# Final norm of a graph layer and expert feed-forward kernel: statistics of the last tile to ScalarE, scaling of tiles four and five to ScalarE and GpSimd's transfers

## What is computed

```python
edge_index = jnp.stack([src, dst])
x = x + _L0_gnn_ref(_layernorm(x, axis=-1), edge_index, W, b)
x = x + _L0_ffn_ref(_layernorm(x, axis=-1)[None], router_w, router_b, w1, b1, w2, b2, ln_w, ln_b)[0]

# the end of _L0_ffn_ref: out is the weighted sum of the experts
out = out.reshape(b, s, h) + hidden_states
return _layernorm(out, ln_w, ln_b)      # eps 1e-12, mean and variance over the 1024 columns
```

## Time and profile before

| what | value |
|---|---|
| median of 3 runs | 615.42 us (614.85 to 615.75) |
| the profiled execution, its own time | 617.8 us |
| its span, first to last instruction | 615.7 us |
| PE, DVE, ACT, POOL busy share of the span | 87%, 75%, 39%, 32% |
| DMA, mean rate over the span | 182 GB/s |
| mean granted TensorE clock | 0.954 of full |
| last expert add issued by GpSimd | 574.61 us |
| last matmul issued | 572.20 us |

### The profile page before, as it was taken

One profiled execution on the slowest core, in us unless ns is written; L12 is line 12 of the kernel. 1 busy time (PEld: TensorE's weight loads), 2 busy tenths in 40 slices (PEclk: granted clock), 3 DMA queues, 4 the chain that ended last, 5 costly groups with the idle time before them and its releaser, 6 DMA issues.

```text
span 615.7 us, 12330 instructions
## 1 busy us (share of the span) xinstructions
PE 533.8 (87%) x3660; PEld 298.8 (49%) x3661; DVE 464.7 (75%) x1295; ACT 243.0 (39%) x358; POOL 194.4 (32%) x199
## 2 busy tenths in 40 slices
PE   1799999899999999995879999999999999999100
PEld 1344554445544555553764655556565656564000
DVE  8889869996185888888748678695868685755397
ACT  5334444323271434342634343444443444401480
POOL 3023000000001375746434535343453444151240
PEclk9999999999999999997789999999999999999755
DMA  6873531243237334346367959698888889273878
GB/s 237 322 289 100 155 89 25 56 78 65 50 140 271 137 139 172 138 171 204 90 262 203 296 164 256 217 238 274 208 251 207 258 230 281 29 168 77 264 209 278
DMA packets 59581, 112.34 MB, mean 182 GB/s; under 512 B 33506, under 2 KB 33919, under 8 KB 59520
## 3 DMA queue, kind: packets, MB, share of 16 engines
q1 hardware_dynamic: 49440, 80.02, 37.4%
q0 software_dynamic: 8896, 27.38, 21.3%
q10 hardware_dynamic: 1184, 4.20, 1.9%
HBM read 71.75 MB, written 33.67 MB: 171 GB/s over the span
## 4 chain that ended last, share of the span: by engine, by line
PE 77%; DVE 14%; issue 4%; DMA 3%; ACT 1%; DVEq 0%; ACTq 0%; SPq 0%; POOLq 0%
PE ps L1818 7%; PE ps L1819 7%; PE ps L1943 7%; PE ps L1944 6%; PE ps L1945 6%; PE ps L1922 6%; PE ps L1923 5%; PE ps L1924 5%; PE ps L1728 5%; PE ps L1729 4%; PE ps L1730 4%; PE ps L1655 4%; PE ps L1904 4%; DMA acc_rows<-work,ids_out 1%; DVE wbufs L1574 1%
## 5 line engine op out<-in xcount | busy, mean ns | idle before, releaser
L615 POOL DMA_INDIRECT acc_rows<-work,ids_out x24 | 53.0, 2206 | 107.6 <-DVE work L1510 107.6
L1922 PE MATMUL ps<-rows_and_counts,wbufs 128*128 128x336 f16 (+2 forms) x256 | 76.1, 301 | 3.0 <-issue 2.2
L1924 PE MATMUL ps<-rows_and_counts,wbufs 128*128 128x336 f16 (+2 forms) x256 | 76.1, 301 | 0.0
L1923 PE MATMUL ps<-rows_and_counts,wbufs 128*128 128x336 f16 (+2 forms) x256 | 76.1, 301 | 0.0
L1819 PE MATMUL ps<-wbufs,rows_and_counts 128*128 128x512 f16 x200 | 75.8, 379 | 0.0
L1818 PE MATMUL ps<-wbufs,rows_and_counts 128*128 128x512 f16 x200 | 75.8, 379 | 0.0
L1943 PE MATMUL ps<-wbufs,rows_and_counts 128*128 (+1 forms) x192 | 72.9, 380 | 1.8 <-issue 1.3
L1465 DVE SCALAR_TENSOR_TENSOR wbufs<-stage,wbufs 128x1024 f16<-128x1024 f32 x56 | 67.1, 1218 | 8.1 <-ACT wbufs L933 7.6
L1944 PE MATMUL ps<-wbufs,rows_and_counts 128*128 (+1 forms) x192 | 72.8, 379 | 0.0
L1945 PE MATMUL ps<-wbufs,rows_and_counts 128*128 (+1 forms) x192 | 72.8, 379 | 0.0
L528 POOL TENSOR_TENSOR work<-work 128x1024 f16<-128x1024 f32 x9 | 19.2, 2132 | 164.3 <-ACT work L906 164.3
(11 more groups left out here) (310 smaller groups left out, 1050.5 us busy)
## 6 DMA issues: line engine op xcount, KB each, us to landing
stage<-wst_in SPq DMA_DIRECT2D x72, 512.0 KB
acc_rows<-work SPq DMA_DIRECT2D x10, 512.0 KB
x_rows<-work SPq DMA_DIRECT2D x10, 512.0 KB
wbufs<-b_in ACTq DMA_DIRECT2D x8, 512.0 KB
wbufs<-acc_rows SPq DMA_DIRECT2D x8, 512.0 KB, 5.9
t<-x_in SPq DMA_DIRECT2D x1, 3584.0 KB, 13.2
t<-x_in SPq DMA_DIRECT2D x1, 3072.0 KB, 11.3
t<-x_in SPq DMA_DIRECT2D x1, 2048.0 KB, 7.8
```

The costliest lines, as they stand in the source:

```text
L1922: mm(o, wbufs[:, ds(w + ws, P)], x_hi, start=(j == 0), stop=False)
L1923: mm(o, wbufs[:, ds(w + ws, P)], x_lo, start=False, stop=False)
L1924: ins = mm(o, wbufs[:, ds(w + (LO + ws), P)], x_hi, start=False, stop=(j == DK - 1))
```

## The change

ScalarE takes the statistics of tile 9 too, so VectorE has no statistics of its own in the third group. `ADDED` grows from tiles 0 to 3 to tiles 0 to 5 and `WHOLE` shrinks to tiles 6 to 9: tiles 4 and 5 are stored as `t` early, scaled by ScalarE at line 1027 and added onto `out` by GpSimd's line 647, and are neither passed over by VectorE's line 1612 nor stored by SyncE's line 745. GpSimd waits for six landed stores of `t` in place of four. Neither the groups nor the order of the waits on the other lines changes.

```diff
-ACT_TILES = (0, 1), (4, 5), (8,)
-ADDED = LAST_GROUPS[0]
-WHOLE = LAST_GROUPS[1] + LAST_GROUPS[2]
+ACT_TILES = (0, 1), (4, 5), (8, 9)
+ADDED = LAST_GROUPS[0] + LAST_GROUPS[1][:2]
+WHOLE = LAST_GROUPS[1][2:] + LAST_GROUPS[2]
...
                 act.wait_ge(rstd5_done, n + 1)
-                for r in tiles:
+                for r in [r for r in tiles if r in ADDED]:
                     act.wait_ge(weighed, r + 1)
                     a.activation(fin[r], fin[r], ACT.Copy, scale=rstd5[:, r:r + 1]).then_inc(scaled, 1)
...
-                own = tiles
-                if n < len(ACT_TILES):
-                    own = tiles[len(ACT_TILES[n]):]
-                cs = slice(own[0], own[-1] + 1)
+                own = tiles[len(ACT_TILES[n]):]
                 for r in own:
                     dve.wait_ge(fin_in[r], 16)
                     st5.did(v.bn_stats(stats5[:, r, 0:6], fin[r][:, 0:HALF]))
                     st5.did(v.bn_stats(stats5[:, r, 6:12], fin[r][:, HALF:D]))
+                if own:
+                    cs = slice(own[0], own[-1] + 1)
+                    st5.wait()
+                    for r in own:
+                        st5.did(v.bn_aggr(mv5[:, r, :], stats5[:, r, :]))
+                    st5.wait()
+                    st5.did(v.tensor_scalar(var5[:, cs], mv5[:, cs, 1], EPS2, None, ALU.add))
+                cs = slice(tiles[0], ACT_TILES[n][-1] + 1)
+                dve.wait_ge(square5_done, n + 1)
+                ins = v.tensor_scalar(var5[:, cs], square5[:, cs], EPS2, None, ALU.add)
                 st5.wait()
...
-                if tiles[0] in WHOLE:
+                if tiles[-1] in WHOLE:
                     dve.wait_ge(x1b_done, NT)
                     dve.wait_ge(rstd5_done, n + 1)
-                    for r in tiles:
+                    for r in [r for r in tiles if r in WHOLE]:
                         dve.wait_ge(weighed, r + 1)
                         v.scalar_tensor_tensor(fin[r], fin[r], rstd5[:, r:r + 1], t[:, r * D:(r + 1) * D],
                                                ALU.mult, ALU.add).then_inc(finished, 1)
```

More of the change, by code:

```diff
@@ L1585, in _ @@
                     st5.did(v.bn_stats(stats5[:, r, 6:12], fin[r][:, HALF:D]))
-                st5.wait()
[L1587 to L1596, removed]
+                if own:
[8 more added lines that the diff above has]
+                ins = v.tensor_scalar(var5[:, cs], square5[:, cs], EPS2, None, ALU.add)
+                st5.wait()
                 ins.then_inc(var5_done, 1)
```

## The result

Six runs of the changed kernel gave a median of 623.70 us (622.57 to 625.25), six of the kernel before 615.59 us (613.46 to 618.07). The ratio is 1.0138 with a 95% interval of 1.0113 to 1.0163: 8.5 us slower, where I had forecast 1.7.

The account below looks back on a forecast made before the run. The DMA engines were to become the bound: two adds cost 5.2 us, two stores fewer give 2.5, and VectorE's 4 us only fill a gap. That made 1.7 us more, 617.1 us, range 615.3 to 618.5.

Parts of the forecast that it names:

- 4.0 us forecast: VectorE in the tail: two final passes fewer give 2.39 us, tile 9's statistics and the first small addition 1.63.
- both covers: ScalarE's slack before VectorE needs its results: 1.8 us for tile 9's sums, 0.9 us for the third group's root.
- the early part: Two more early stores of `t` on SyncE: forecast to cost nothing, at most 1 us by delaying GpSimd's expert-weight gathers.
- the fourth rival: Early stores push the gathers past VectorE's read, last expert's results up to 1 us late: 618.1 us, chance 0.07.
- the queue never runs dry: GpSimd's queue: tile 4's add is queued by 604.7, while the fourth add runs until 607.1; issue time costs nothing.
- 23.2 us to the last byte: DMA engines: data end at 616.25, counted from the first add's issue at 593.07.
- the price of an add: DMA engines: an accumulating tile takes 2.6 us at 0.20 MB/us, a plain store 1.25 us.
- the filled gap: The DMA engines' wait for VectorE between 611.1 and 612, under one us, was to be filled with work.
- The 1.2 us: Stretch from the last data at 614.54 to the span's end at 615.7, carried over unchanged to the changed kernel.
- my own sum: DMA work after 603.4: 1.58 MB of adds (7.8 us) plus 2.10 MB of stores (5.05 us), 12.85 us.
- the reading from which I began: Two resources nearly level in the tail, VectorE and the DMA engines; the change relieves the first and loads the second.
- The faster rival: Adds hold the DMA engines no longer than plain stores, VectorE's 4.0 us come off in full: 611.4 us, chance 0.08.

## Why the prediction was right in its direction and wrong in its size

VectorE: right. 4.0 us forecast and 4.02 found.

ScalarE: right. Its statistics, scalings and root came, set against the first add's issue, within 0.1 us of the forecast, and both covers held.

SyncE and the early part: the two early stores were put at nothing, with up to 1 us as the other end, and cost 0.6 us ahead of the tail. The path wasn't the one forecast: VectorE's read of the expert weights isn't late, TensorE's matmul of line 1943 is. Of the fourth rival the effect came true, the last expert's results late, and not its cause.

GpSimd's issues: the two new ones began 8.8 and 11.2 us after the first, forecast 9.6 and 11.9. I had given them a start-up of 1.1 us that only the first has. But "the queue never runs dry" was wrong, as the fifth add's data didn't move until 605.7.

The DMA engines: the size was right, 23.2 us to the last byte forecast and 23.4 found; so were the price of an add (2.6 us of engine time, with 0.42 MB/us for the plain transfers as the contrast) and the filled gap. That the total came out within 0.2 us is in part luck, as the order was another: tiles 8 and 9 weren't stored beside the adds from 604.16 on, but 4.7 us later.

The step that failed is the one behind it: "Now they end at 614.54 and the span at 615.7, 1.2 us later. So the span becomes 616.25 + 1.2." I took SyncE's last store for the only end, because the chain of waits closed on VectorE's last pass, whose result that store carries, and SyncE's last long wait was for that store. The 1.2 us held GpSimd's drain, which ended 0.4 us after SyncE's stream by coincidence, having begun at 608.2. That drain follows the last add, not the last byte. Put into my own sum it gives the result: the adds' data would end at about 603.4 + 1.58/0.143 = 614.5 (0.143 MB/us being the adds' share of both queues, 0.53 MB in 3.7 us), they land 0.9 us later as before (607.1 to 608.0), and 7.7 us on the span ends at 623.1, 7.4 over before against 8.1 found. Of the 0.7 left, 0.5 is a later landing and 0.2 a longer way from landing to end (7.9 us in place of 7.7); whether the pause is behind the 0.5 isn't shown. So of a loss of 8.1 us in the tail, my mechanism, the engines' work, carries 2.0 (the last byte), and the drain that had been hidden behind VectorE and the stores carries 6.1.

The same row overturns the reading from which I began. It was not VectorE and the DMA engines that were level in the tail of the kernel before, but SyncE's end, which both of these feed, and GpSimd's. None of my rivals had the second. The upper end of the range, 618.5, contained only rates and the early part, and nothing for a second end. The faster rival is settled: adds don't move at the plain rate, alone or shared.

## What to carry to other kernels

Before costing an edit in the last microseconds, list when each engine's stream ends and what it does there, drains included, since they count as idle in every view of busy time; an end that is hidden by half a us is a second bound. If GpSimd issues transfers late, let another engine wait for their landing and let GpSimd go straight to its end (3.6 us in the changed kernel), and give late work to transfers that don't accumulate. Sum the work of the DMA engines by kind, and then ask as well which queue's last transfer the end depends on, for a full engine says nothing of the order in which the queues are served.

## What the runs showed of the hardware that I had not expected

GpSimd's closing DRAIN took 7341 ns with four late transfers (the kernel before and the versions with four adds in which GpSimd waits), 7422 with five and 7504 with six, all landed and waited for: 7.0 us and some 81 ns for each transfer, if these three values lie on a line. Begun while transfers were under way, it ended 3.9 to 4.1 us after the last one landed. What GpSimd does in it, no row shows.

An accumulating transfer moved 0.20 MB/us with the engines full, a plain one of the same form and queue 0.42.

With six adds, GpSimd's queue stood nearly still for 1.4 us between the fourth and the fifth, whose data began to move 6.8 us after its issue, where the first add's took 2; and SyncE's stores of the last two tiles moved 4.7 us after their issue, where those of the kernel before took 0.8 with both queues empty. The pause of GpSimd's queue appeared in every kernel with five or six of these transfers, 1.2 to 1.4 us long, with the two plain ones too. Its cause stays open.

Two more early stores of 0.524 MB, which kept the DMA engines busy 2.6 us longer (59.5% against 39.6% of a 13 us window), delayed a TensorE matmul by 0.6 us, although it reads nothing of them. Its cause stays open too.
